# VectorE takes two row maxima per instruction; FFN weights move to other key buffers; the last chunk is stored tile by tile

## The reference

```
x = x + attention(layernorm(x))     # 16 heads of width 32; scores/sqrt(32) + 0.1 where |i-j| <= 2; softmax over 2048 keys
x = x + linear(layernorm(x))        # 512 x 512
```

## Time and profile before

| | |
|---|---|
| median of 3 runs | 4154.99 us (4146.64 to 4157.97) |
| profiled execution | 4162.25 us, its span 4160.4 us |
| PE busy | 4039.1 us, 97% |
| DVE busy | 3363.4 us, 81% |
| POOL busy | 3031.1 us, 73% |
| ACT busy | 2407.6 us, 58% |
| mean granted TensorE clock | 0.991 |

### The profile page before, as it was taken

The page is one execution under the profiler, slowest core; times in us unless marked ns, Lnnn a source line. Parts: engine busy times, 40 slices in busy tenths (PEclk is TensorE's granted clock), DMA queues, the critical chain, the costliest instruction groups (busy, mean ns, idle before and its releaser), DMA issues.

```text
span 4160.4 us, 59566 instructions
## 1 busy us (share of the span) xinstructions
PE 4039.1 (97%) x21328; PEld 2537.2 (61%) x21328; DVE 3363.4 (81%) x5630; ACT 2407.6 (58%) x4651; POOL 3031.1 (73%) x1118
## 2 busy tenths in 40 slices
PE   8999999999999999999999999999999999987998
PEld 6788875555555555555555555555555555546877
DVE  6444568888888888888988888888888898867887
ACT  2122216766667667767676766776676767662332
POOL 2111108888988888889888888988888888974542
PEclk9999999999999999999999999999999999998999
DMA  7888759899999999999999999999999899986664
GB/s 246 264 265 255 231 158 180 182 213 189 200 199 193 200 192 205 188 211 185 210 185 212 189 199 200 194 200 192 203 188 208 181 212 185 210 193 170 178 168 102
DMA packets 292270, 825.16 MB, mean 198 GB/s; under 512 B 28832, under 2 KB 95392, under 8 KB 229536
## 3 DMA queue, kind: packets, MB, share of 16 engines
q0 software_dynamic: 72960, 486.57, 59.4%
q1 hardware_dynamic: 219040, 335.09, 28.9%
HBM read 211.82 MB, written 156.24 MB: 88 GB/s over the span
## 4 chain that ended last, share of the span: by engine, by line
PE 74%; DVE 15%; ACT 3%; POOL 3%; DMA 3%; issue 2%; SPq 0%; POOLq 0%; ACTq 0%; DVEq 0%
PE ps_a L872 19%; PE ps_a L858 19%; PE ps_b L837 16%; PE ps_p L481 12%; DVE part_max L1049 9%; PE ps_b L903 3%; DVE p_sb L1076 3%; POOL pair L1218 3%; PE ps_b L950 2%; ACT p_sb L1025 2%; PE ps_b L883 1%; DMA pair<-pair 1%; PE ps_a L933 1%; DMA k_odd<-wd_lo_d 1%; DMA q_st<-shift 0%
## 5 line engine op out<-in xcount | busy, mean ns | idle before, releaser
L1049 DVE TENSOR_REDUCE part_max<-ps_b 128x1 f32<-128x512 f32 x4016 | 2465.0, 680 | 375.5 <-PE ps_b L837 375.3
L1025 ACT ACTIVATE p_sb<-ps_a 128x512 f32<-128x512 f32 x4096 | 2083.6, 614 | 723.7 <-PE ps_a L858 719.5
L1218 POOL TENSOR_TENSOR pair<-p_sb 128x2048 f32<-128x2048 f32 x512 | 2454.1, 4813 | 65.7 <-ACT p_sb L1025 61.9
L872 PE MATMUL ps_a<-p_sb,v_sb 128*32 128x512 f32 x8192 | 995.8, 603 | 38.7 <-DVE p_sb L1076 21.9
L858 PE MATMUL ps_a<-q_st,k_odd 97*128 97x512 f32 x2048 | 843.9, 415 | 7.0 <-DMA q_st<-shift 3.8
L858 PE MATMUL ps_a<-q_st,k_even 97*128 97x512 f32 x2048 | 844.5, 412 | 5.3 <-PEq L163 3.8
L837 PE MATMUL ps_b<-k_odd,q_st 96*128 96x512 f32 x2048 | 813.2, 397 | 0.0
L837 PE MATMUL ps_b<-k_even,q_st 96*128 96x512 f32 x1968 | 783.0, 398 | 0.0
L858 PEld LDWEIGHTS ps_a<-q_st,k_odd 97*128 97x128 f32 x2048 | 387.6, 190 | 332.7 <-issue 214.3
L858 PEld LDWEIGHTS ps_a<-q_st,k_even 97*128 97x128 f32 x2048 | 387.7, 189 | 320.8 <-issue 219.4
L872 PEld LDWEIGHTS ps_a<-p_sb,v_sb 128*32 128x32 f32 x8192 | 224.4, 109 | 523.8 <-ACT p_sb L1025 319.9
(11 more groups left out here) (113 smaller groups left out, 2862.1 us busy)
## 6 DMA issues: line engine op xcount, KB each, us to landing
pair<-pair POOLq DMA_DIRECT2D x448, 1024.0 KB, 8.9
q_st<-q_hi_d SPq DMA_DIRECT2D x128, 256.0 KB, 7.1
xin<-in_x SPq DMA_DIRECT2D x16, 1024.0 KB, 8.7
xb_d<-xb SPq DMA_DIRECT2D x16, 1024.0 KB, 5.6
q_hi_d<-s_hi SPq DMA_DIRECT2D x64, 256.0 KB, 6.2
q_lo_d<-s_lo SPq DMA_DIRECT2D x64, 256.0 KB, 7.1
k_hi_d<-s_hi SPq DMA_DIRECT2D x64, 256.0 KB, 3.4
k_lo_d<-s_lo SPq DMA_DIRECT2D x64, 256.0 KB, 4.3
```

Of the source, the lines that this page charges most:

```text
L872: last = nc.tensor.matmul(ps_a[h * HD:(h + 1) * HD, RING_S, :], v_sb[:, kt, h * HD:(h + 1) * HD], p_sb[:, s % SLOTS, h, :], start=(kt == 0 ...
L1025: nc.scalar.activation(p_sb[:, s % SLOTS, h, :], ps_s[:, (HG * s + h) % RING_S, :], ACT.Exp, scale=SCALE).then_inc(p_ready, 1)
L1049: nc.vector.tensor_reduce(part_max[:, unit % 2, col, n:n + 1], ps_m[:, max_place(unit, j) % RING_M, :], AX.X, ALU.max).then_inc(max_taken, 1)
L1218: nc.gpsimd.tensor_tensor(pair[:, m % PAIR_RING], p_sb[:, s % SLOTS], p_sb[:, (s + 1) % SLOTS], ALU.add).then_inc(paired, 1)
```

## The change

`with_next(unit, j)` is true where j sits in an even place, j+1 in the next place (so that both banks lie side by side), and both belong to the same block of keys. There DVE skips j, and at j+1 reduces both banks by one instruction, which writes two columns of `part_max` and then adds 2 to `max_taken`. The linear layer's weights go to `k_odd` blocks 0 and 1 and are loaded in the last unit at steps 6 and 9; `o_lo[1]` goes to block 2. The second last chunk's residual sums move behind the last chunk's rounding, and the last chunk is stored in four DMAs of one tile.

```diff
+    def with_next(unit, j):
+        return (j + 1) % (HG * TT) > 0 and max_place(unit, j) % 2 == 0 and max_place(unit, j + 1) == max_place(unit, j) + 1
...
-        o_hi, o_lo = (k_even[:, 0], q_st[:, 1]), (q_st[:, 2], k_odd[:, 0])
-        wo_hi, wo_lo, wd_hi, wd_lo = k_even[:, 2], k_even[:, 3], k_odd[:, 1], k_odd[:, 2]
+        o_hi, o_lo = (k_even[:, 0], q_st[:, 1]), (q_st[:, 2], k_odd[:, 2])
+        wo_hi, wo_lo, wd_hi, wd_lo = k_even[:, 2], k_even[:, 3], k_odd[:, 0], k_odd[:, 1]
...
-                    if unit == NU - 1 and kt == 9:
+                    if unit == NU - 1 and kt in (6, 9):
                         sp.wait_ge(scored, HG * (s - 1))
-                        sp.dma_start(f32(wd_hi), wd_hi_d).then_inc(wd_in, 16)
+                        n = (kt - 6) // 3
+                        sp.dma_start(f32((wd_hi, wd_lo)[n]), (wd_hi_d, wd_lo_d)[n]).then_inc(wd_in, 16)
...
             load_rec(2)
-            sp.wait_ge(scored, HG * ST)
-            sp.dma_start(f32(wd_lo), wd_lo_d).then_inc(wd_in, 16)
             sp.wait_ge(pv_done, ST)
...
             def take(unit, j):
-                n, col = j // (HG * TT), j % (HG * TT)
+                if with_next(unit, j):
+                    return
+                two = 2 if j > 0 and with_next(unit, j - 1) else 1
+                first = j + 1 - two
+                n, col, bank = first // (HG * TT), first % (HG * TT), max_place(unit, first) % RING_M
                 v.wait_ge(max_scored, max_no(unit, j) + 1)
-                nc.vector.tensor_reduce(part_max[:, unit % 2, col, n:n + 1], ps_m[:, max_place(unit, j) % RING_M, :],
-                                        AX.X, ALU.max).then_inc(max_taken, 1)
+                nc.vector.tensor_reduce(part_max[:, unit % 2, col:col + two, n], ps_m[:, bank:bank + two, :],
+                                        AX.X, ALU.max).then_inc(max_taken, two)
...
                 if kt == 12:
+                    v.wait_ge(scored, HG * (KT * (NU - 1) + 3 * TT))
                     o_low(1)
...
-                    quantise(c + 1, lambda j: [last_sum(c, t) for t in ((0,), (1, 2), (3,))[j]])
+                    parts = ((0,), (1, 2), (3,)) if c + 2 < NCH else ((), (), (0, 1))
+                    quantise(c + 1, lambda j: [last_sum(c, t) for t in parts[j]])
                 else:
+                    for t in (2, 3):
+                        last_sum(c - 1, t)
                     for t in range(TT):
                         last_sum(c, t)
...
-            for c in range(NCH - 3, NCH):
+            for c in range(NCH - 3, NCH - 1):
                 store(c)
+            c = NCH - 1
+            for t in range(TT):
+                pool.wait_ge(res_ready, TT * c + t + 1)
+                pool.dma_start(out_ch[c][:, t, :], res[c % 2][:, t, :], accum_op=ALU.add).then_inc(out_done[c % 2], 16)
```

More of the change, by code:

```diff
@@ L811, in _ @@
                     store_rec(NG - 1)
-            for i in range(2):
-                sp.wait_ge(out_done[i], 16 * (NCH // 2))
+            sp.wait_ge(out_done[0], 16 * (NCH // 2))
+            sp.wait_ge(out_done[1], 16 * (NCH // 2 - 1 + TT))
             sp.wait_ge(o_out, 16 * NU)
```

## The result

The changed kernel takes 4534.67 us (median of 4 runs, 4531.02 to 4538.93) against 4156.48 us for the kernel before, whose median now has a fourth run in it: ratio 1.0909, 95% interval 1.0893 to 1.0925. It is slower, as forecast, but by 378 us where 285 were forecast, and the time lies above the range (4380 to 4485).

What follows compares the result with a forecast made beforehand. PE was taken to bound the kernel, with DVE following. From the profiled 4162 us, +300 for attention, -10 for FFN weights and -6 for last stores gave 4446, or 4440 us against the median; range 4380 to 4485.

Steps and rivals of the forecast that it cites:

- What bounds the kernel, and which way it goes: Attention: PE sets the time, DVE follows; couples make the four-bank ring two places deep; slower, chance 0.92.
- Six full periods: Periods of four couples, j from 14 on: PE held 0.38 and 0.19 us, 0.57 each, 3.4 us a unit.
- taken off for places where PE waits already: About 0.2 us a unit of the stalls lie where PE already waits, at band work and key sums.
- The five full periods: Full periods of four couples other than the one from j = 14 on: 0.57 us more each, 177 us in all.
- The period with (1,2): Period of 62, 63, 0 single, then (1,2), (3,4) and 5: M7 (j = 5) starts 0.45 us late.
- DVE comes to (1,2) late (rows before it, L1054): In that period DVE starts (1,2) about 2.4 us after M0 and ends at 3.6, delaying j = 5 by 0.45 us.
- The period across the burst: Period of 6, 7, turned maxima, 8 to 13: j = 8 late by 0.77 us, 12 by 0.38, sum 1.15 us.
- The turned maxima: They stand between 7 and 8 in the period across the burst; no cost was put on their coming later.
- Nothing behind it becomes tight: Behind the slower attention, ACT, POOL and the DMAs get 10% more room; no added cost.
- The stalls cost clock as well: Rival: granted clock falls to 1.2 GHz once a unit, another 1.7 us a unit, 4545 us; chance 0.03.
- The FFN weights: After attention: earlier weight loads spare PE's 11.3 us wait at the first linear layer; gain 4 to 14, taken -10 us.
- The last stores: Kernel's end: stores by tile -4 us, chunk 14's sums moved -2 us; together -6 us (-2 to -9).

Runs made afterwards that it cites:

- e2_late: Changed kernel with couples only for j from 8 on, in the second half of a period; ratio 0.9996 to the kernel before.
- e3_early: Changed kernel with couples only for j from 8 on, in the first half of a period; ratio 1.0552 to the kernel before.
- e4 to e6: Changed kernel with single reductions: banks given back by twos (1.0325), DVE starting by twos (1.0316), both (1.0976); ratios to the kernel before.
- e11_ffn_only: Kernel before with only the FFN weights' edit; ratio 0.9996 to the kernel before.
- e7_from8: Changed kernel with couples only for j from 8 on, none below; 4389.93 us, ratio 1.0583 to the kernel before.
- e4_joint: Changed kernel with single reductions started as each maximum is in, two banks given back together; ratio 1.0325 to the kernel before.

## Why the prediction was wrong

- **What bounds the kernel, and which way it goes:** right. PE sets the time, DVE's busy time doesn't matter, and a ring of four banks that is emptied by twos holds PE at the fifth and the seventh maximum. e2_late against e3_early, and e4 to e6, show it.
- **Six full periods:** the mechanism was right, the term 0.57 us was too small for the usual period; it measured 0.66 (6.47 against 5.81). The sum let the two-bank step start 0.43 us after the second maximum and last 1.21; it started after 0.50 and lasted 1.23.

Of the 93 us between the 285 forecast and the 378 measured, 88 are attention's. What the terms came to shows when attention is cut at the first maximum after each burst, and the 62 or 63 periods of a kind are summed in the two profiled executions (us; the forecast is for 62 units):

| period | before | after | more | forecast |
|---|---|---|---|---|
| from j = 62 on, with (1,2) | 362.5 | 421.8 | 59.3 | 28 |
| from j = 6 on, across the burst | 370.2 | 449.3 | 79.1 | 71 |
| from j = 14 on (full) | 366.7 | 433.7 | 67.0 | 35 |
| the five other full ones | 1927.8 | 2109.0 | 181.2 | 177 |
| taken off for places where PE waits already | | | | -12 |
| sum | | | 386.6 | 299 |

- **The five full periods** are on average only 0.58 us longer, as PE stood in some of them before as well. That is 16 us over the sum's 177 - 12.
- **The period with (1,2):** this failed, at "DVE comes to (1,2) late (rows before it, L1054)". The sum put 0.45 us on it in every unit, behind L1054 alone. It missed the order on DVE: band work stands between j = 1 and j = 2, and in every fourth unit it comes before the couple. There PE stands 1.4 us before j = 5, and the period is 2.3 us longer on average (8.33 against 6.00, with the clock's falls in it); in the other units it is 0.5 longer, as the sum had it. In all it is 31 us over the sum. The period across the burst measured 1.28 us where 1.15 were put: 8 us.
- **The turned maxima:** this failed as well, at "Nothing behind it becomes tight". They come later behind the couples, and PE's waits for the shift's DMA rise from 14 to 69 us over weight loads and matmuls, which overlap in part. The period where they fall, from j = 14 on, is 1.6 us longer in one unit of four at the median, 0.66 of it as in any full period, and costs 32 us over the sum in all. The sum had nothing for it.
- **"The stalls cost clock as well"** was a rival with 0.03, priced at one fall in every unit, 4545 us. The measured time lies close to that number, but by chance: the clock's falls are 9 in all and cost about 15 us of 378, and they came behind holes of 1.3 us and more, not behind those of 0.4.
- **The FFN weights:** -10 was taken, nearer to the wait removed. The next late thing, chunk 2's load, left less than even the other bound, 4 us: 1.5 us at the second linear layer, nothing measurable in e11_ffn_only. **The last stores:** -6 was taken; 2.8 us came from the store by tiles (a tile takes 6.7 us to land where 5 was taken) and 1.5 from the earlier rounding (the last two linear layers start 14.5 us apart, before 16.1). The end's 10.7 us in the one profile hold some us that differ from run to run; over 12 runs the end's edits give 7 where 16 were forecast.

## What to carry to other kernels

Before two instructions on a ring's reader are merged, work out when each buffer comes back, and not what the reader saves: merging delays the first start by one item and the first release by one more, and a ring of four becomes a ring of two. Such merging is free where the buffers are wanted late (here just ahead of a burst), and could gain something where the reader is the bound, which no run here shows. If other work stands between the two items on the reader's queue, it now comes before both.

## What the runs showed of the hardware

A reduction over two PSUM banks takes 1.22 us (1221 ns, the mean of 1881 in the changed kernel) where two single ones in a row take 1.28. The table of the Trainium skill ("VectorE: DVE Perf Modes", trn2 errata) gives an estimate of 1.19, 2% less; its rule to minimise the number of operations ("Rules for kernel authors") holds for DVE's busy time here, which fell by 125 us, and the kernel got slower by following it. The two-bank reduction started 0.50 us after the start of the matmul it waited for, single ones 0.43 to 0.44; why is open. Holes of 0.1 to 0.6 us in each full period left TensorE's granted clock at 2.4 GHz (e7_from8). After single holes of 1.3 to 2.7 us it fell to 1.2 GHz for 3.4 or 6.8 us, in some units and not in others: 8 times of 15 in the change and never of 15 in e4_joint, at holes of the same place and nearly the same length.
